# Two graph-attention layers on one core: every buffer behind the weight matrices starts 32 bytes further on

## The reference

```python
# layer 0: 12 heads of 64
h = einsum('bnd,ade->bane', x, W);  th = tanh(h)
attn = th @ w_src + swapaxes(th @ w_dst);  attn = where(attn >= 0, attn, 0.2 * attn)
attn = softmax(where(~adj, -999, attn))
feat = elu(attn @ h + b);  gate = sigmoid(x @ H_w.T + H_b)
x = layernorm(x + gate * feat + (1 - gate) * x)
# layer 1: 6 heads of 128
q, k, v = x @ Wq + bq, x @ Wk + bk, x @ Wv + bv
probs = softmax(q @ k.T / sqrt(128) + where(adj, 0, -9e15))
x = layernorm(x + (probs @ v) @ Wf + bf)
```

## Time and profile before

| | |
|---|---|
| median of 3 runs | 2842.39 us (2838.29 to 2844.92) |
| profiled execution | 2836.27 us |
| its span, first to last instruction | 2834.5 us |
| mean granted TensorE clock in it | 0.997 |
| TensorE matmul busy | 2807.6 us, 99% |
| weight loads busy | 2590.4 us, 91% |
| VectorE busy | 1718.8 us, 61% |
| ScalarE busy | 1056.6 us, 37% |
| GpSimd busy | 474.6 us, 17% |

### The profile page before, as it was taken

The page is one execution under the profiler, slowest core; times in us unless marked ns, Lnnn a source line. Parts: engine busy times, 40 slices in busy tenths (PEclk is TensorE's granted clock), DMA queues, the critical chain, the costliest instruction groups (busy, mean ns, idle before and its releaser), DMA issues.

```text
span 2834.5 us, 52061 instructions
## 1 busy us (share of the span) xinstructions
PE 2807.6 (99%) x21696; PEld 2590.4 (91%) x21696; DVE 1718.8 (61%) x3334; ACT 1056.6 (37%) x2597; POOL 474.6 (17%) x264
## 2 busy tenths in 40 slices
PE   8999999999999999999999999999999999999998
PEld 6778888888888899999999999999999999999998
DVE  7898998888888864454444444444444444444443
ACT  4555555455545532322322233322332223223322
POOL 1211111111111122111212121212221121212120
PEclk9999999999999999999999999999999999999999
DMA  4434443333333421112111111112111221121110
GB/s 158 141 104 122 141 130 101 108 113 108 102 108 113 142 85 64 48 46 68 57 57 46 60 65 57 46 52 70 60 46 46 68 66 48 46 68 57 57 35 23
DMA packets 117162, 221.91 MB, mean 78 GB/s; under 512 B 38080, under 2 KB 54464, under 8 KB 116928
## 3 DMA queue, kind: packets, MB, share of 16 engines
q1 hardware_dynamic: 116928, 218.59, 24.2%
HBM read 142.65 MB, written 75.89 MB: 77 GB/s over the span
## 4 chain that ended last, share of the span: by engine, by line
PE 97%; DVE 2%; DMA 0%; issue 0%; ACT 0%; DVEq 0%; SPq 0%
PE ps_hg L884 28%; PE ps_k L69 15%; PE ps_a L1038 14%; PE ps_q L69 14%; PE ps_a L69 14%; PE ps_s L988 2%; PE ps_c L1020 2%; PE ps_pv L919 2%; PE ps_t L872 1%; PE ps_t L906 1%; PE ps_pt L1020 1%; PE ps_pt L995 1%; PE ps_q L951 1%; PE ps_s L951 0%; PE ps_k L951 0%
## 5 line engine op out<-in xcount | busy, mean ns | idle before, releaser
L884 PE MATMUL ps_hg<-w_hi,xT 128*128 128x512 f32 x2280 | 766.9, 404 | 7.2 <-DVE h_one L663 4.3
L884 PEld LDWEIGHTS ps_hg<-w_hi,xT 128*128 128x128 f32 x2280 | 430.3, 189 | 107.2 <-issue 5.1
L884 PE MATMUL ps_hg<-w_lo,xT 128*128 128x512 f32 x1140 | 451.8, 396 | 0.0
L69 PE MATMUL ps_k<-x1T_hi,wk_hi 128*128 128x256 f32 x1152 | 328.5, 285 | 0.0
L516 ACT ACTIVATE qT<-ps_q,bq_col 128x256 f32<-128x256 f32 x192 | 80.5, 470 | 661.2 <-PE ps_q L69 661.2
L69 PE MATMUL ps_q<-x1T_hi,wq_hi 128*128 128x256 f32 x1152 | 322.4, 280 | 2.0 <-DVE x1T_lo L757 2.0
L69 PE MATMUL ps_q<-x1T_lo,wq_hi 128*128 128x256 f32 x1152 | 322.1, 280 | 0.0
L69 PE MATMUL ps_q<-x1T_hi,wq_lo 128*128 128x256 f32 x1152 | 322.0, 280 | 0.0
L69 PE MATMUL ps_k<-x1T_lo,wk_hi 128*128 128x256 f32 x1152 | 321.5, 279 | 0.0
L69 PE MATMUL ps_k<-x1T_hi,wk_lo 128*128 128x256 f32 x1152 | 321.3, 279 | 0.0
L69 PE MATMUL ps_a<-wv_hi,x1T_hi 128*128 128x384 f32 x768 | 264.4, 344 | 0.0
(11 more groups left out here) (133 smaller groups left out, 5322.1 us busy)
## 6 DMA issues: line engine op xcount, KB each, us to landing
x_tok<-x SPq DMA_DIRECT2D x64, 384.0 KB, 3.4
dst_all<-dst_scratch SPq DMA_DIRECT2D x128, 192.0 KB, 3.3
gate_scratch<-gate SPq DMA_DIRECT2D x64, 384.0 KB, 3.4
feat_scratch<-feat SPq DMA_DIRECT2D x128, 192.0 KB, 2.8
feat_in<-feat_scratch SPq DMA_DIRECT2D x62, 384.0 KB, 3.1
gate_in<-gate_scratch SPq DMA_DIRECT2D x62, 384.0 KB, 3.7
x_even<-x SPq DMA_DIRECT2D x16, 768.0 KB, 4.4
x_odd<-x SPq DMA_DIRECT2D x16, 768.0 KB, 4.5
```

Source lines behind the costliest of these rows:

```text
L69: ins = pe.matmul(out, left[a][c], right[b][c], start=(n == 0), stop=(n == len(terms) - 1))
L884: ins = pe.matmul(ps_hg[:, cols], left[a][c], right[b][c], start=(c == 0 and n == 0), stop=(c == KC - 1 and n == 2))
```

## The change

Two lines are changed. The base is rounded up to a multiple of 64 where it was rounded up to a multiple of 32, and S is 832 bytes plus x_even's size behind BOTH where it was 800 plus that size. x_even itself stays at BOTH + 800.

```diff
-        base = -(-nc.sbuf_base // 32) * 32
+        base = -(-nc.sbuf_base // 64) * 64
...
         x_even = at(BOTH + 800, "x_even", [P, GT, D])
...
-        S = BOTH + 800 + GT * D * 4
+        S = BOTH + 832 + GT * D * 4
         xT = at(S, "xT", [P, 2, 2, KC, P], F32R)
```

## The result

The changed kernel takes 2850.19 us (median of 8 runs, 2845.05 to 2851.82), the kernel before 2841.27 us (median of 8, 2838.29 to 2844.92). The ratio is 1.0033, 95% interval 1.0023 to 1.0043: 9 us slower. The forecast was no change, 2842 us. The time lies inside the range given, at its slow end, but the likeliest case was wrong.

What follows compares the result with a forecast made beforehand. TensorE, busy 2807.6 of 2834.5 us, was taken as the bound. The only nonzero term, 1 us gained in q and k, gave 2835.3 us from the profiled 2836.3, or 2841.4 by the median, rounded to 2842; range 2830 to 2851.

Steps and rivals of the forecast that it cites:

- the likeliest case: Whole kernel: no change beyond what a measurement can tell, 2842 us, own range 2837 to 2848, chance 0.79.
- What bounds the kernel: Whole kernel: TensorE is busy 2807.6 of 2834.5 us; a product costs the distance between starts, not its latency.
- Stationary operand onto the multiple: Weight loads from xT and x1T already take 188 to 189 ns, like those from wq and wk; gain 0 us.
- Moving operand onto the multiple: Layer 1's 6912 q and k matmuls of 256 columns: 116.7 to 116.6 ns, a gain of 1 us.
- First rival: All big products: the 9% above 0.4167 ns a column is one operand off the multiple; 201 us gain, 2641 us, chance 0.03.
- The estimate of 162 us: Big products: gain if the skill's rule of N / 2.4 + 2.5 ns a matmul were fulfilled, giving 2680 us.
- Second rival: q and k products: only the moving operand matters, gaining 5.5 to 13.8 us, 2837 to 2828 us; chance 0.08.
- Third rival: Big products: stationary and moving reads at the same remainder modulo 64 slow each other, 19.5 us, 2862 us; chance 0.05.
- Its objection to itself: Big products: moving addresses step by 1 KB and more and loads run at no fixed distance, so no lasting step arises.
- Its price of 1.3 ns: Excess of context matmuls over transposes, charged on all 14976 matmuls, 19.5 us.
- Small TensorE work, ScalarE and VectorE, transfers: Context matmuls, probsT loads, operations on moved buffers and tile loads: each taken as 0 us.
- The list of what would show it: Trace signs for each case: q and k pieces 4.20 us if right, 4.13 if only the moving operand matters.

Runs made afterwards that it cites:

- e2: The changed kernel with its base 32 bytes up, so matrices and x1T both lie 32 past a multiple of 64; 2848.34 us, 1.0039 times the kernel before.
- e3: The kernel before with everything from S moved up by 64 bytes, remainders by 64 kept; 2861.4 us, 1.0080 times the kernel before.
- e5: The kernel before with xT, x1T_hi and x1T_lo 32 bytes down, x_even also 32 down, seed sharing tmp; 2847.18 us in one timed run.
- e4: TensorE alone on constant data at the kernel's addresses, moving and stationary buffers shifted in 32-byte steps, three matmul forms; 512-column matmuls took 233.3 to 226.7 ns.
- e11: The kernel before with everything from S moved up by 128 bytes; 2852.45 us in a single timed run.
- e6: The kernel before with xT 32 bytes down and x1T left in place, x_even and the small seed buffer moved for room; 2824.39 us, ratio 0.9946.
- e1: The changed kernel with xT, x1T_hi and x1T_lo alone put back to their earlier places; 2841.01 us, 1.0012 times the kernel before.
- e7: The kernel before with xT 32 bytes down, x1T_hi and x1T_lo 96 down, x_even 128 down, small statistics packed; 2816.86 us, ratio 0.9919.
- e8: TensorE alone on constant data, 40 blocks of 72 matmuls, weight-load widths, buffer shifts and lead-in matmuls varied; one q distance gave 113.3 or 117.8 ns by lead.

## Why the prediction was wrong

*What bounds the kernel* held, and so did the reading by distances between starts. It is what made the 1.1 ns visible at all.

*"Stationary operand onto the multiple ... 0 us"*: the loads kept their 188 to 189 ns, and layer 0, whose stationary operand moved onto the multiple, kept its 233.3 ns. Right for these; output changed by no more than 1.4 us. For the values it failed by 1.9 us (3.18 for 3.13 in the first 18).

*"Moving operand onto the multiple ... I take the 512-column rate, a gain of 1 us"* is the step that failed. In place of a gain of 1 us, q and k lost 1.1 ns a matmul, 6.3 us summed over the trace. The failure is not the size alone: the moving operand's multiple of 64 has no effect of its own (e2, e3), its distance from the stationary one has. I compared forms (256 against 384 and 512 columns) whose x buffers stand at one and the same distance from their matrices, 32 bytes modulo 256, and read from their equal rates that a shift of 32 bytes does nothing. The earlier trace rows hold no second distance, so they could not say it: what e3 and e5 show for q and k at other distances, 4.32 us, is outside all that I extrapolated from. The kernel before did have one second distance, that of cT and wf in output, and it ran at the rate of the values (344 ns in the earlier trace rows for both); it would have misled in the same way, since the cost at a distance is another for each form.

*First rival* (9% is the price of one operand off): refuted by the change itself, which runs all three forms with both on the multiple at 0.457 to 0.460 ns a column (4.21 us for 18 of 512, 3.18 for 18 of 384, 4.24 for 36 of 256). The estimate of 162 us beside it comes to 164 by its own factors. Part of the 9% is to be had, though by another distance: 226.7 ns for 512 columns in e4 is 0.4427 ns a column, 6% above 0.4167.

*Second rival* (only the moving operand): wrong sign for q and k.

*Third rival* (both reads of TensorE in step) had the right pair of operands and the right sign, and 0.05 of the chance. The sign was luck: at -32 bytes the remainders by 64 are the same as at +32, and there layer 0 becomes faster (4.10 us for 4.20 in e5). It took the wrong modulus: by e3 and e11, the remainder by 64 of before gives 4.32 and 4.22 us for 4.20. Its objection to itself, that addresses which step by 1 KB leave no lasting step, was wrong: steps of 1 KB are multiples of 256, so that they keep the relation. Its price of 1.3 ns on all 14976 is near for q and k (1.1) by chance, since it came from two small forms, and wrong for the others.

*Small TensorE work, ScalarE and VectorE, transfers*: 0 each, as measured within the profile: context pieces 0.89, ps_pv 0.86, output's wait for cT_lo 6.5 us. That VectorE was not in the way in layer 0 held even when the tile became 0.2 us shorter in e6: in the stretch from 100 to 900 us TensorE is busy for 798.4 us there, 798.8 before.

*The chances*: 0.80 for no change rested on a single distance. The list of what would show it named the right piece (q and k, 4.20) and only the wrong direction (4.13). Its last test, a big product whose distance moves by 0.4 ns or more, was met by 1.1.

What stays open: what has the period of 256 bytes; why the distances settle on values such as 113.3, 116.7 and 120.0 ns; what picks one of two rhythms where no lead does; what shifts of less than 32 bytes do, which no run tried; and most of the 0.1% that e1 keeps.

## What to carry to other kernels

Where TensorE is the bound and every matmul has a weight load of its own, as here, the place of the moving buffer relative to the stationary one is a free parameter. In this kernel it was worth 0.9913 to 1.0080 of the time. Sweep it in steps of 32 bytes over 256, each product for itself, and not as an alignment. Try the best places in the kernel itself, since a rhythm that a long block settles into may be lost in the entry of a block of 18, or hold in every second group only. Judge it by the distance between starts, which shows 0.04 us in a piece of 4.20 where the run's time scatters by 0.2%, and over all groups: one group of e7 has 4.24 us and the next 4.08. And when several forms agree in a rate, ask first whether they differ in the quantity that the change will alter.

## What the hardware showed that I had not expected

- Moving x1T against its matrices by 32, 64, -32, -96 and 128 bytes changes 36 q or k matmuls from 4.20 to 4.24, 4.32, 4.32, 4.24 or 4.08, and 4.22 us.
- A matmul of 512 columns goes from 233.3 to 226.7 ns by a shift of 32 bytes, and one of 256 columns from 116.7 to 120.0 by the same shift; over all distances it lies between 113.3 and 120.0.
- The same matmuls at the same addresses have more than one stable rhythm: output pieces in e6 alternate between 12.67 and 12.87 us from group to group, q and k in e7 between 4.08 and 4.24, and in e8 four short matmuls ahead of a block make it 113.3 ns for 117.8.
- Narrower weight loads (64 or 32 columns for 128) make the matmuls behind them sometimes slower: 226.7, 230.0, 231.7 ns in the layer 0 form at (0,32).
